# Graph layers with two gates on one core: 29 first additions of the gates as accumulating DMAs, and five smaller moves

## The chip, the cores and the metric

One NeuronCore of a Trainium2 chip runs the whole program. The metric is the device time of one execution in microseconds; the time before is the median of three runs, 809.16 us (806.93 to 809.22).

## What is computed

`x` has 256 nodes of 768 features. Four blocks follow each other, each as `x = x + block(relu(layernorm(x)))`: two relational graph layers with a gate behind each (L0), three relational graph layers (L1), a small attention network with an MLP (L2), and a two-layer attention network (L3). The change is almost wholly in the two gates of L0:

```python
def _gate(h, q, Wg, bg, Wq, bq):          # h: 8 x 32 nodes x 768, q: 8 x 64 x 768
    hg = jnp.einsum('bnf,gf->bng', h3, Wg[:, :F])
    qg = jnp.einsum('blf,gf->blg', q, Wg[:, F:]) + bg
    attn = jax.nn.sigmoid(hg[:, :, None, :] + qg[:, None, :, :])
    qi = jnp.einsum('bnlf,blf->bnf', attn, q)
    alpha = jax.nn.sigmoid(jnp.einsum('bnf,gf->bng', h3, Wq[:, :F])
                           + jnp.einsum('bnf,gf->bng', qi, Wq[:, F:]) + bq)
    return alpha * jnp.tanh(qi) + (1.0 - alpha) * h3
```

For each of 8 batches, 32 nodes, 64 query rows and 768 features one sigmoid is taken, multiplied by a query value and summed over the 64 rows.

## The kernel before

**A gate** (i = 0 after the first relational layer, i = 1 after the second) runs 48 steps. A step `s` takes 128 features of one batch, features on the partitions, and handles 32 nodes x 64 query rows = 2048 values, as two halves `u` of 1024 (32 rows `l` each):

- TensorE (`arguments`) makes hg + qg in PSUM with a selection matrix, two matmuls of 512 columns for each half.
- ScalarE (`sigmoid`, L864) writes the sigmoids of both halves to one of six product tiles, `slot_view(s)` (tile `s % 6`).
- VectorE (`gate_product`, L2050) multiplies all 2048 values by the query, which a copy holds in PSUM bank 6.
- GpSimd (`first_fold`, L640) adds the second half to the first: 1024 values are left. Step 47 alone is reduced by VectorE directly (L2057).
- What then happens is set for each step by a letter of `KIND[i]`. `V`: VectorE reduces 1024 values to 32 (`reduce`, L2072). `G`: GpSimd halves once more (`second_fold`, L646), VectorE reduces 512. `H`: GpSimd halves twice (L646, L649), VectorE reduces 256. `T`: TensorE adds in PSUM (`fold`, 8 calls of an identity matmul that appear as 16 rows of L1490), VectorE reduces 128.

Every engine works through its own list in order. The lists are written by hand in tables: `FOLD_AT[i]` (before which TensorE step a `T` is folded), `SECOND_AT[i]` (after which first addition GpSimd does a second one), `REST_AT[i]` (after which product VectorE does which reductions). `BY_DMA[i]` names steps whose first addition is made by a DMA that adds its source to its destination; before, both lists are empty. A product tile is free for step `s + 6` when its first addition is done (for half 1) and when it is reduced (for half 0); for a `T` the fold is enough.

**Beside the steps** TensorE makes the gate's own projections (`beside`): heads, query rows, `own` (h times Wq) and `query_part` (qi times Wq), which share two PSUM banks `acc`. They go to ScalarE and VectorE as high and low parts in `stage_hi` and `stage_lo`, from where SP's queue spreads them into `HQ` (`spread_heads`, `spread_queries`). At step 34 ScalarE takes the sigmoid of the first 128 nodes' update weight from `acc` into the SBUF tile `alpha` (`gate_alpha`, L883), VectorE multiplies (`gate_scale`, L2084), and GpSimd adds (`gate_add`, L655 or L658). From step 36 TensorE starts on `acc` anew with the other 128 nodes (`own(1, ...)`, bias matmul L1112). Their weight is handled behind step 47 (`last_half`, L2098).

**Weights** come as slabs of 768 KB through a ring of four, on SP's queue (L526), each issued when the slab four places ahead has been used. ScalarE's queue carries the vectors of the attention blocks, broadcast to all partitions (`av`, 2 MB, L915, issued at step 25 of the second gate), and the biases (L958) behind the second gate. `av` is first read behind the second relation of the third layer.

In L2's first attention layer VectorE makes two groups of columns of logit weights for the next layer (`logit_weights`, L2163 and L2167) between the two halves of `rows_lo(0, t)` (L2263), which TensorE's logits wait for.

## Time and profile before

| | |
|---|---|
| median of 3 runs | 809.16 us |
| profiled execution, its own time | 807.43 us |
| its span, first to last instruction | 805.6 us |
| first gate, steps from 114 to 262 us | 148 us |
| second gate, steps from 325 to 471 us | 146 us |
| TensorE matmul busy | 776.0 us (96%) |
| VectorE busy | 604.2 us (75%) |
| GpSimd busy | 508.5 us (63%) |
| ScalarE busy | 423.8 us (53%) |
| granted TensorE clock, mean | 0.999 |

The share of busy time over the span mixes the gates with the layers' products around them, which are bound otherwise. The gates have to be read by themselves: busy time of each engine within their two windows, the waits there, and the pace at which each engine goes from step to step. An instruction's mean duration in the list of groups includes a small overlap with the next one on its engine.

### The profile page before, as it was taken

The page shows a single profiled execution, that of the slowest core. Times are in us where ns is not written, and L with a number is a line of the kernel's source. Part 1 is how long each engine was busy: PE and PEld are TensorE (multiplying, and loading weights), DVE is VectorE, ACT ScalarE, POOL GpSimd, SP SyncE. Part 2 cuts the span into 40 slices and gives each one's busy share as a digit, 9 for nine tenths or more (in the row PEclk, how much of TensorE's full clock was granted, in tenths as well). Part 3 has the DMA queues.
Part 4 walks back from the last instruction along what each step waited for, and adds up shares of the span by engine and source line. Part 5 has one row for each costly group of instructions (what it writes and reads, how often), then busy time and mean ns, then how long its engine had stood idle before and what let it go on. Part 6 is the DMA issues. An engine that isn't in the chain of part 4 may idle for free.

```text
span 805.6 us, 10743 instructions
## 1 busy us (share of the span) xinstructions
PE 776.0 (96%) x4278; PEld 649.8 (81%) x4278; DVE 604.2 (75%) x664; ACT 423.8 (53%) x508; POOL 508.5 (63%) x216
## 2 busy tenths in 40 slices
PE   7999999999999999999999999999999999998998
PEld 4669995677756699667867768999999999975897
DVE  8966249999999740899999988564895498567454
ACT  6424446777675342677776734435442454253742
POOL 0535609999999274699999945750784177805500
PEclk9999999999999999999999999999999999999999
DMA  9037425445332474270344328465365446350001
GB/s 366 37 79 235 159 77 165 108 146 156 119 118 79 130 231 150 53 208 1 121 155 141 109 101 301 160 207 185 124 202 181 159 157 204 110 236 1 1 1 40
DMA packets 24410, 111.03 MB, mean 138 GB/s; under 512 B 3620, under 2 KB 6180, under 8 KB 23976
## 3 DMA queue, kind: packets, MB, share of 16 engines
q1 hardware_dynamic: 23240, 104.24, 39.9%
q10 hardware_dynamic: 1120, 6.10, 2.0%
q8 instruction: 34, 0.56, 0.3%
q14 instruction: 16, 0.13, 0.0%
HBM read 100.63 MB, written 0.79 MB: 126 GB/s over the span
## 4 chain that ended last, share of the span: by engine, by line
PE 68%; DVE 21%; POOL 4%; ACT 4%; issue 2%; DMA 0%; DVEq 0%; ACTq 0%
PE ps L1152 27%; DVE prod L2050 13%; PE ps L1118 10%; PE ps L1183 6%; PE ps L1443 5%; DVE qi_t L2072 4%; PE ps L1490 4%; PE ps L1665 3%; POOL w_lo L624 2%; PE ps L1310 2%; PE ps L1331 2%; ACT prod L864 2%; PE ps L1733 1%; PE ps L1311 1%; PE ps L1380 1%
## 5 line engine op out<-in xcount | busy, mean ns | idle before, releaser
L624 POOL TENSOR_TENSOR w_lo<-w_raw,w_hi 128x1536 fp32r<-128x1536 f32 x49 | 185.3, 3794 | 138.6 <-ACT w_hi L731 138.5
L640 POOL TENSOR_TENSOR prod<-prod 128x1024 f32<-128x1024 f32 x94 | 222.7, 2396 | 30.1 <-DVE prod L2050 29.8
L864 ACT ACTIVATE prod<-ps 128x1024 f32<-128x1024 f32 x192 | 185.8, 1024 | 64.9 <-PE ps L1443 63.8
L2050 DVE TENSOR_TENSOR prod<-prod,ps 128x2048 f32<-128x2048 f32 x96 | 216.9, 2281 | 1.4 <-ACT prod L864 1.0
L731 ACT ACTIVATE w_hi<-w_raw 128x1536 fp32r<-128x1536 f32 x60 | 88.9, 1487 | 119.0 <-PE ps L1152 108.6
L1443 PE MATMUL ps<-sel_pair,h_and_q 128*128 128x512 f32 x384 | 125.8, 442 | 10.5 <-ACT prod L864 9.8
L1152 PE MATMUL ps<-w_hi,yt_hi 128*128 128x384 f32 x480 | 122.9, 336 | 1.2 <-POOL w_lo L624 1.2
L1152 PE MATMUL ps<-w_lo,yt_hi 128*128 128x384 f32 x480 | 121.9, 334 | 0.0
L1152 PE MATMUL ps<-w_hi,yt_lo 128*128 128x384 f32 x480 | 121.8, 334 | 0.0
L1118 PE MATMUL ps<-w_raw,h_t 128*128 128x384 f32 x312 | 106.5, 486 | 0.0
L1443 PEld LDWEIGHTS ps<-sel_pair,h_and_q 128*128 128x128 f32 x384 | 66.6, 189 | 42.2 <-ACT prod L864 19.8
L1152 PEld LDWEIGHTS ps<-w_hi,yt_hi 128*128 128x128 f32 x480 | 85.4, 188 | 2.1 <-POOL w_lo L624 2.1
L1152 PEld LDWEIGHTS ps<-w_lo,yt_hi 128*128 128x128 f32 x480 | 86.8, 188 | 0.0
L1152 PEld LDWEIGHTS ps<-w_hi,yt_lo 128*128 128x128 f32 x480 | 86.7, 188 | 0.0
L1118 PEld LDWEIGHTS ps<-w_raw,h_t 128*128 128x128 f32 x312 | 58.7, 189 | 34.3 <-issue 0.2
L1937 DVE TENSOR_TENSOR ps<-ps,rinv 128x512 f32<-128x512 f32 x54 | 36.8, 695 | 55.9 <-PE ps L1183 55.3
L1490 PEld LDWEIGHTS ps<-prod,ident 128*128 128x128 f32 x544 | 65.8, 192 | 4.5 <-DVE qi_t L2072 0.4
L1490 PE MATMUL ps<-prod,ident 128*128 128x128 f32 x544 | 66.2, 275 | 0.0
L731 ACT ACTIVATE yt_hi<-ps 128x512 fp32r<-128x512 f32 (+1 forms) x58 | 35.0, 612 | 41.0 <-DVE ps L1937 40.6
L1924 DVE TENSOR_TENSOR w_lo<-w_raw,w_hi 128x1536 fp32r<-128x1536 f32 x11 | 20.9, 1904 | 43.5 <-ACT w_hi L731 43.3
L2072 DVE TENSOR_REDUCE qi_t<-prod 128x32 f32<-128x1024 f32 (+2 forms) x60 | 53.5, 901 | 0.0
L1183 PE MATMUL ps<-a,h_hi 128*128 128x256 f32 x192 | 48.1, 290 | 0.9 <-DVE yt_lo L1941 0.9
(263 smaller groups left out, 1110.0 us busy)
## 6 DMA issues: line engine op xcount, KB each, us to landing
w_raw<-weights SPq DMA_DIRECT2D x105, 768.0 KB, 4.4
wa_in<-weights SPq DMA_DIRECT2D x6, 768.0 KB, 5.9
w_gat<-weights SPq DMA_DIRECT2D x6, 768.0 KB, 9.2
w_query<-weights SPq DMA_DIRECT2D x3, 768.0 KB, 11.4
h_and_q<-stage_hi SPq DMA_DIRECT2D x24, 96.0 KB, 2.1
h_and_q<-stage_lo SPq DMA_DIRECT2D x24, 96.0 KB, 2.2
a_vec<-gat_vectors ACTq DMA_DIRECT2D x1, 2048.0 KB, 9.3
q_t<-queries ACTq DMA_DIRECT2D x1, 1536.0 KB, 10.3
```

What stands on the lines that cost most here:

```text
L624: pool.tensor_tensor(Wl[:, j, :], raw_slab(U, 0, j), Wh[:, j, :], ALU.subtract).then_inc(w_lo_by_pool, 1)
L640: pool.tensor_tensor(v[:, 0], v[:, 0], v[:, 1], ALU.add).then_inc(folded_once, 1)
L731: return act.activation(o, i, ACT.Copy)
L864: act.activation(slot_view(s)[:, u], args.rearrange("p b (n l) -> p (b n) l", l=LH), ACT.Sigmoid).then_inc(sigmoid_ready, 1)
L1118: return pe.matmul(ps[:, bank + h, 0:FH], left, raw_slab(U, c, k // 2)[:, o:o + FH], start=start, stop=stop)
L1152: mm = pe.matmul(ps[:, bank + h, 0:FH], Y[:, s, k, t * P:(t + 1) * P], Wx[:, j, c0:c0 + FH], start=False, stop=(last and k == KC - 1 and n ...
L1183: ins = pe.matmul(ps[:, 4 + j, kk * N:(kk + 1) * N], Hx[:, t, k * P:(k + 1) * P], A[:, t, v - 1, :], start=(n == 0), stop=(n == 3))
L1443: mm = pe.matmul(ps[:, bank + h, :], HQ[:, b, u, f * P:(f + 1) * P], SEL[:, h * 512:(h + 1) * 512], start=True, stop=True)
L1490: mm = pe.matmul(o, ident[:], slot_view(s)[:, 0, :, 4 * k:4 * k + 4], start=(k == 0), stop=(k == 7))
L1937: TT(tile3(j), tile3(j), inverse.unsqueeze(1).broadcast_to([P, 2, N]), ALU.mult).then_inc(sums_scaled, 1)
L2050: TT(slot_view(s), slot_view(s), query, ALU.mult).then_inc(products_ready, 1)
L2072: dve.tensor_reduce(qiT[:, f, b * NB:(b + 1) * NB], terms, AX.X, ALU.add).then_inc(qi_ready, 1)
```

## The change

- **29 first additions by DMA**: `BY_DMA` names 14 steps of the first gate and 15 of the second. GpSimd issues the DMA in place of the addition; who needs the result waits for the DMA's semaphore (`wait_folded`).
- **Sums dealt anew**: all tables. The kinds V, G, H, T number 17, 10, 6, 14 before and 11, 13, 11, 12 now in the first gate, 13, 10, 4, 20 before and 9, 12, 10, 16 now in the second. Of the steps that go by DMA, 9 and 6 are V, 2 and 3 G, 1 and 1 H, 2 and 5 T. Twenty of the 29 are reduced four products after their own, three (steps 1 and 3 of the first gate, 23 of the second) after three, and six (8, 30, 36 of the first gate, 17, 21, 30 of the second) after five.
- **Update weight in PSUM**: the sigmoid is written over its argument in `acc`, and VectorE multiplies from there; TensorE waits for that product before it starts on `acc` again. The tile `alpha` is gone.
- **Second pair of staging tiles** for the third group of query rows (`query_stage(2)`), at the addresses of `tq` and the former `alpha`; `gate_diff` therefore waits for the spread of that group.
- **Vectors' broadcast** at step 44 of the second gate instead of 25.
- **Logit weights of L2's second layer** in two calls, with `rows_lo(0, 1)` between them.

```diff
-BY_DMA = [(),
-          ()]
+BY_DMA = [(1, 3, 8, 11, 14, 19, 24, 27, 30, 34, 36, 38, 41, 44),
+          (3, 12, 14, 16, 17, 19, 21, 23, 25, 30, 33, 35, 38, 41, 44)]
...
-        alpha = sb("alpha", [P, F], F32, y_off + 15360)
+        second_lo = sb("second_stage_lo", [P, F], F32R, y_off + 12288)
+        second_hi = sb("second_stage_hi", [P, F], F32R, y_off + 15360)
...
+        def query_stage(r):
+
+            return (second_hi, second_lo) if r == 2 else (stage_hi, stage_lo)
...
-                if r == 2:
+                if r == 3:
                     act.wait_ge(lower_spread, 128)
-                if r == 3:
-                    act.wait_ge(query_spread[2], 128)
-                copy(halves(stage_hi[:]), two_banks(bank)).then_inc(staged_hi, 1)
+                copy(halves(query_stage(r)[0][:]), two_banks(bank)).then_inc(staged_hi, 1)
...
-                    act.activation(halves(alpha[:]), two_banks(acc), ACT.Sigmoid).then_inc(alpha_ready, 1)
+                    act.activation(two_banks(acc), two_banks(acc), ACT.Sigmoid).then_inc(alpha_ready, 1)
...
-                    if s == 25 and i == 1:
+                    if s == 44 and i == 1:
                         act.dma_start(av[:], gavec.partition_broadcast(P)).then_inc(vectors_in, 16)
...
                         if s == 36:
-                            pe.wait_ge(alpha_ready, 3 * i + 1)
+                            pe.wait_ge(alpha_diff_ready, 3 * i + 1)
...
-                    TT(tq[:], tq[:], alpha[:], ALU.mult).then_inc(alpha_diff_ready, 1)
+                    TT(halves(tq[:]), halves(tq[:]), two_banks(acc), ALU.mult).then_inc(alpha_diff_ready, 1)
...
-            logit_weights(1, raw_slab(30, 0, 1)[:, 0:2 * N], 0, 2, True)
+            logit_weights(1, raw_slab(30, 0, 1)[:, 0:2 * N], 0, 2, False, (0,))
             rows_lo(0, 1)
+            logit_weights(1, raw_slab(30, 0, 1)[:, 0:2 * N], 0, 2, True, (1,))
```

GpSimd's list in the first gate, from the first addition of step 7 on. `prod_N` is one of the six product tiles; before:

```order
L640 TENSOR_TENSOR prod_101<-prod_101 128x1024 [waits products_ready]
L646 TENSOR_TENSOR prod_101<-prod_101 128x32x16 [waits folded_once]
L640 TENSOR_TENSOR prod_102<-prod_102 128x1024 [waits products_ready]
L640 TENSOR_TENSOR prod_103<-prod_103 128x1024 [waits products_ready]
L640 TENSOR_TENSOR prod_104<-prod_104 128x1024 [waits products_ready]
L640 TENSOR_TENSOR prod_105<-prod_105 128x1024 [waits products_ready]
L646 TENSOR_TENSOR prod_105<-prod_105 128x32x16 [waits folded_once]
L649 TENSOR_TENSOR prod_105<-prod_105 128x32x8 [waits folded_twice]
```

and now:

```order
L646 TENSOR_TENSOR prod_102<-prod_102 128x1024 [waits products_ready]
L652 TENSOR_TENSOR prod_102<-prod_102 128x32x16 [waits folded_once]
L643 DMA prod_103<-prod_103 128x1024 [waits products_ready]
L646 TENSOR_TENSOR prod_104<-prod_104 128x1024 [waits products_ready]
L646 TENSOR_TENSOR prod_105<-prod_105 128x1024 [waits products_ready]
L652 TENSOR_TENSOR prod_105<-prod_105 128x32x16 [waits folded_once]
L655 TENSOR_TENSOR prod_105<-prod_105 128x32x8 [waits folded_twice]
L643 DMA prod_106<-prod_106 128x1024 [waits products_ready]
L652 TENSOR_TENSOR prod_103<-prod_103 128x32x16 [waits dma_folded2]
```

Steps 8 and 11 have become a DMA each, and the second addition of step 8 stands three first additions later, behind a wait for its transfer, with the rest of GpSimd's list behind it.

VectorE's list in the first gate around the scaling at step 34, before:

```order
L2050 TENSOR_TENSOR prod_104<-prod_104,ps 128x2048 [waits sigmoid_ready]
L2072 TENSOR_REDUCE qi_t<-ps 128x32 [waits fold_ready]
L2072 TENSOR_REDUCE qi_t<-prod_102 128x32 [waits folded_once]
L2084 TENSOR_TENSOR tanh_q<-tanh_q,alpha 128x768 [waits alpha_ready,diff_ready]
L2050 TENSOR_TENSOR prod_105<-prod_105,ps 128x2048 [waits sigmoid_ready]
```

and now:

```order
L2054 TENSOR_TENSOR prod_105<-prod_105,ps 128x2048 [waits sigmoid_ready]
L2076 TENSOR_REDUCE qi_t<-prod_102 128x32 [waits folded_thrice]
L2090 TENSOR_TENSOR tanh_q<-tanh_q,ps 128x768 [waits alpha_ready,diff_ready]
L2054 TENSOR_TENSOR prod_106<-prod_106,ps 128x2048 [waits sigmoid_ready]
L2076 TENSOR_REDUCE qi_t<-ps 128x32 [waits fold_ready]
```

One short reduction instead of two stands ahead of the scaling, and the scaling's second operand is in PSUM.

TensorE's list at step 36 of the first gate, where `acc` is started anew, before:

```order
L1443 MATMUL ps<-sel_pair,h_and_q 128x512
L1112 MATMUL ps<-bias,sel_row 128x384 [waits alpha_ready]
L1112 MATMUL ps<-bias,sel_row 128x384
L1118 MATMUL ps<-w_raw,h_t 128x384 [waits w_landed0]
L1118 MATMUL ps<-w_raw,h_t 128x384 x2
```

and now:

```order
L1447 MATMUL ps<-sel_pair,h_and_q 128x512
L1116 MATMUL ps<-bias,sel_row 128x384 [waits alpha_diff_ready]
L1116 MATMUL ps<-bias,sel_row 128x384
L1122 MATMUL ps<-w_raw,h_t 128x384 [waits w_landed0]
L1122 MATMUL ps<-w_raw,h_t 128x384 x2
```

The same matmuls now wait for VectorE's scaling, no longer for ScalarE's sigmoid; the sigmoid arguments of step 37 stand behind them.

## Rows read from the trace of the kernel before

**Rows 1.** Windows: length; busy PE, PEld, DVE, ACT, POOL; clock; DMA share; GB/s.
```profile
114.00:262.00 148.00, 141.62 (x646) 101.43 (x645) 147.01 (x110) 102.70 (x115) 137.68 (x70) 1.00 0.42 121
325.00:471.00 146.00, 138.69 (x695) 102.39 (x693) 143.02 (x114) 103.91 (x117) 135.73 (x68) 1.00 0.36 110
262.00:283.00 21.00, 20.65 (x100) 14.77 (x101) 14.44 (x19) 8.34 (x11) 6.07 (x2) 1.00 0.46 144
```
**Rows 2.** Groups by form, first gate: count, busy, mean ns, idle before.
```profile
L640 POOL TENSOR_TENSOR prod<-prod 128x1024 f32<-128x1024 f32 x47 | 110.8, 2390 | 22.1 <-DVE prod L2050 21.9
L646 POOL TENSOR_TENSOR prod<-prod 128x512 f32<-128x512 f32 x16 | 21.3, 1328 | 1.3
L649 POOL TENSOR_TENSOR prod<-prod 128x256 f32<-128x256 f32 x6 | 4.4, 736 | 0.5
L2072 DVE TENSOR_REDUCE qi_t<-prod 128x32 f32<-128x1024 f32 x17 | 20.6, 1213 | 0.0
L2072 DVE TENSOR_REDUCE qi_t<-prod 128x32 f32<-128x512 f32 x10 | 6.7, 676 | 0.0
L2072 DVE TENSOR_REDUCE qi_t<-prod 128x32 f32<-128x256 f32 x6 | 2.5, 415 | 0.0
L2072 DVE TENSOR_REDUCE qi_t<-ps 128x32 f32<-128x128 f32 x14 | 4.0, 287 | 0.0
L2084 DVE TENSOR_TENSOR tanh_q<-tanh_q,alpha 128x768 f32<-128x768 f32 x1 | 2.0, 2035 | 0.0
L1975 DVE TENSOR_TENSOR stage_lo<-ps,stage_hi 128x768 fp32r<-128x768 f32 x3 | 2.9, 952 | 0.0
```
**Rows 3.** The same view, second gate.
```profile
L640 POOL TENSOR_TENSOR prod<-prod 128x1024 f32<-128x1024 f32 x47 | 111.9, 2403 | 8.0 <-DVE prod L2050 7.9
L2072 DVE TENSOR_REDUCE qi_t<-ps 128x32 f32<-128x128 f32 x20 | 5.8, 288 | 1.9 <-PE ps L1490 1.9
L2084 DVE TENSOR_TENSOR tanh_q<-tanh_q,alpha 128x768 f32<-128x768 f32 x1 | 1.2, 1182 | 0.0
L629 POOL TENSOR_TENSOR small<-small,mhalf 128x1 f32<-128x1 f32 x1 | 0.6, 570 | 0.0
```
**Rows 4.** Timeline of TensorE, first gate: start, duration, one fold and its step.
```profile
178.47 1.95 PE L1490 MATMUL ps<-prod,ident 128*128 128x128 f32 x16
180.18 1.18 PE L1443 MATMUL ps<-sel_pair,h_and_q 128*128 128x512 f32 x4
```
**Rows 5.** DMA issues of the page: KB each, median us from issue to landing.
```profile
w_raw<-weights SPq DMA_DIRECT2D x105, 768.0 KB, 4.4
a_vec<-gat_vectors ACTq DMA_DIRECT2D x1, 2048.0 KB, 9.3
g_bias<-gat_biases ACTq DMA_DIRECT2D x1, 1536.0 KB, 6.1
```
**Rows 6.** Timeline of SP's queue, the spread of the first heads.
```profile
119.65 0.68 SPq L548 DMA_DIRECT2D h_and_q<-stage_hi  x1
...
129.91 0.60 SPq L548 DMA_DIRECT2D h_and_q<-stage_lo  x1
```
**Rows 7.** Timelines of TensorE and VectorE at step 36, second gate.
```profile
427.56 0.51 PE L1112 MATMUL ps<-bias,sel_row 128*128 128x384 f32 x2
...
427.79 1.18 DVE L2084 TENSOR_TENSOR tanh_q<-tanh_q,alpha 128x768 f32<-128x768 f32 x1
```
**Rows 8.** Timelines: ScalarE at step 44, second gate; a slab load; its use by TensorE.
```profile
453.27 1.96 ACT L864 ACTIVATE prod<-ps 128x1024 f32<-128x1024 f32 x2
...
460.19 0.33 SPq L526 DMA_DIRECT2D w_raw<-weights  x1
...
472.46 2.74 PE L1118 MATMUL ps<-w_raw,h_t 128*128 128x384 f32 x8
```
**Rows 9.** Timelines of VectorE and TensorE in L2's first attention layer.
```profile
715.21 0.28 DVE L2263 TENSOR_TENSOR logit_rows<-ps,logit_rows 40x128 fp32r<-40x128 f32 x1
...
715.55 0.48 PE L1700 MATMUL ps<-sel_dst,logit_rows 128*128 128x512 f32 x1 [0.46 <-DVE logit_rows L2263]
```

40 lines of the change are left out of this document (22 added, 18 removed), and 10 rows, old and new, of the table REST_AT.

## Prediction

> **What bounds the kernel now.** I read the windows of the gates first. VectorE is busy 147.0 of the first gate's 148 us and 143.0 of the second's 146; TensorE 141.6 and 138.7; GpSimd 137.7 and 135.7 [rows 1]. The reader is to see three nearly full engines with VectorE ahead. A cut on one engine is therefore worth only what the other two let through, and has to be made on all three. The groups by form tell what a sum costs on each: VectorE reduces a V in 1.213 us, a G in 0.676, an H in 0.415, a T in 0.287; GpSimd's first addition takes 2.390, a second 1.328, a third 0.736 [rows 2]. A fold lengthens TensorE's step by 180.18 - 178.47 = 1.71 us [rows 4]. A step takes 148/48 = 3.08 us on average. The granted clock stays at 1.00 throughout [rows 1], so the 2.4 GHz level is not in question.
>
> **VectorE.** First gate: six V fewer, three G more, five H more, two T fewer: -7.28 + 2.03 + 2.08 - 0.57 = -3.7 us [rows 2]. Second: four V fewer, two G and six H more, four T fewer. With the same durations and 0.288 for a T [rows 3], that is -4.85 + 1.35 + 2.49 - 1.15 = -2.2 us. The scaling at step 34 has both operands in SBUF and takes 2.035 us in the first gate, 1.182 in the second [rows 2, 3]. With one operand in PSUM, the nearest row of its size takes 0.952 [rows 2]. So -1.1 and -0.2 us. Together: **-4.8 and -2.4 us**.
>
> **TensorE.** Two and four folds fewer: 2 x 1.71 = -3.4 and 4 x 1.71 = -6.8 us. In the first gate TensorE has 6.4 us free, so this mainly keeps it from becoming the bound. In the second VectorE is idle 3.0 us, of which 1.9 are waits for folds [rows 1, 3]; with a fifth fewer folds and the other engines shorter I take back 1.0 us of it (between 0 and 1.9).
>
> **GpSimd.** Without the price of issuing: first gate, 14 first additions fewer, eight second and five third ones more: -33.5 + 10.6 + 3.7 = -19.2 us. Second: 15 fewer, eight and six more, by the same rows: -35.8 + 10.6 + 4.4 = -20.8 us. What an accumulating DMA holds GpSimd for is in no row. From below, GpSimd's smallest operation, 128x1, takes 0.57 us [rows 3]; from above, the addition that it replaces, 2.39. SP's queue holds its engine 0.60 us for one transfer [rows 6]. I take 0.57 + 0.60 = 1.17 us, near the lower end, since writing a list of 128 rows touches far less than adding 131,072 values. Then GpSimd changes by -19.2 + 14 x 1.17 = -2.8 and -20.8 + 15 x 1.17 = -3.3 us. It breaks even at 19.2/14 = 1.37 and 20.8/15 = 1.39 us; its free 10 us per gate [rows 1], about half of them ahead of the first product, cover a little more. The Trainium skill (DMA: Bandwidth & Descriptors, Latency and other measured facts) puts GpSimd's emission at about 1 us; no row shows it, and by it GpSimd would gain 5.2 and 5.8 us, with the sum unchanged because VectorE sets it.
>
> **Landing.** A transfer has a source and a destination of 512 KB each and reads both and writes one: 1536 KB. The row with that many bytes landed after 6.1 us; 768 KB took 4.4, 2048 KB 9.3 [rows 5]. I take 6.1, with 4.4 and 9.3 as bounds. GpSimd is up to 1.3 us behind, by one second addition, and issues for 1.17: ready 8.6 us behind the product. Reduced four products later it has 4 x 3.08 = 12.3 us, three later 9.2. So 26 of 29 are hidden even at 9.3 (11.8 us). The three with lag three are not, at that end, and step 1 of the first gate meets the 16 spread transfers of 119.65 to 130.51 [rows 6]. Product tiles come free for the sigmoids of six steps later, so the same slack covers ScalarE. Seven second additions now wait for a DMA, with the rest of GpSimd's list behind them. Three stand three products after their own, four (34 and 41 of the first gate, 14 and 33 of the second) only two: 2 x 3.08 + 1.17 = 7.3 us, just what issue and landing take together. At 9.3 us those four hold GpSimd 3.2 us each, 6.4 per gate, about its free time. For the three short lags and these four I charge **+0.8 us** together (0 to 3 x 2.6 = 7.8). The skill (same page, Anatomy of one DMA — SWDGE (gpsimd) path) gives 2.0 us plus bytes over 436e3. For 512 KB that would be an estimated 3.2 us, and 5.6 for 1536 KB; no row has a transfer of this kind. By either the 0.8 would fall to 0.
>
> **The other parts.** TensorE's new wait at step 36: in the second gate it started the bias matmul at 427.56, and the scaling began at 427.79 [rows 7]. Ending 0.95 us later it would hold TensorE for 427.79 + 0.95 - 427.56 = 1.2 us, and the sigmoid arguments of step 37 behind it. But of the reductions ahead of it in VectorE's list a T and a G are gone there (a T and a V, for an H, in the first gate), 0.29 + 0.68 us; that leaves **+0.2 us** (0 to 1.2 in each gate), and VectorE is two products away from needing those arguments. `last_half` gets its factor from PSUM: some 0.1 us per product, behind which TensorE is busy 20.65 of 21.00 us [rows 1]; 0. The second pair of staging tiles takes away waits that do not occur before; 0, and the new wait of the difference at step 29 is for transfers issued some 15 steps earlier. The broadcast: ScalarE comes to step 44 at 453.27 [rows 8]; from about 454 2 MB land in 9.3 us alone [rows 5], beside the slab of 460.19, which TensorE needs at 472.46 [rows 8]; even both in a row, 4.4 + 9.3 = 13.7 us from 454, are there by 468. Its first reader stands behind the second relation of the next layer. 0 us, and what it did at step 25 is also hidden. The logit split: `rows_lo` need not wait for the second half of the weights, and TensorE's idle 0.46 us before the logits goes [rows 9]: **-0.4 us**.
>
> **Sum.** -4.8 - 2.4 - 1.0 + 0.8 + 0.2 - 0.4 = -7.6 us on the profiled execution's 807.43 us (span 805.6 and 1.8 around it): 799.8. That execution is 1.7 us below the median of 809.16, so against the median 801.6; I say **802**.
>
> **Rivals.**
> *A, the forecast*: VectorE keeps the lead and gains show. For it: the three engines' cuts are of like size. Best case, issue below 1.2, no late landing, all 3.0 us of idle in the second gate gone: -4.8 - 5.4 - 0.4 = -10.6, 798.5; worst, 3 us more of waits than charged: 804.6.
> *B, GpSimd eats the gain*: at 1.6 us per issue it is +3.2 us longer in both gates (-19.2 + 22.4, -20.8 + 24.0). It starts some 5 us into the gate and has perhaps 3 us of slack there, so the gates end within 1 to 2 us of where they do now: against the median again 807 to 811. That price lies between the row of 0.57 and the row of 2.39, so it can't be excluded.
> *C, GpSimd becomes the bound and the kernel is slower*: one mechanism, the issue of an accumulating DMA in GpSimd's list, from about 1.6 us up. At 2.0 us GpSimd has +8.8 and +9.2 us; less 3 to 5 us of slack each, +9 us together: 818. Against it: SP's 0.60 per transfer.
> *D, late landings*: the DMA engines add at a lower rate than they copy. It decides where landing, waiting and issue exceed 12.3 us, so from 12.3 - 2.5 = 9.8 us. At 10.5 us 26 transfers cost 0.7 each and three 3.8: +30 on top of -8: 831. For it: slab loads and additions meet on engines already 0.42 and 0.36 busy [rows 1], and four of GpSimd's second additions have no slack beyond 6.1 us. Against it: no copy row is that slow.
> That the change does not do what it says is excluded: GpSimd's list has the 29 DMAs in place of the additions.
>
> **Chances.** A measurement of this kernel tells 0.3% (2.4 us) from no change. A 0.69, of which 0.66 faster and 0.03 within; B 0.11 within; C 0.11 and D 0.09 slower. So 0.66 faster, 0.14 the same, 0.20 slower. The range reaches from 797.5 (A's best case and a little of the runs' own spread) up through B to the near part of C: 797.5 to 813. D and the far part of C are left out, about 0.14, and 0.04 below.
>
> **What would show it.** The first gate takes 144 us and the second 142 to 143. VectorE is still busy over 98% of the first. A V among the DMA steps shows no wait of VectorE for a DMA, except at steps 1 and 3 of the first gate. The DMA queue of GpSimd shows 29 issues of 512 KB with a landing near 6 us, and GpSimd's rows leave gaps of about 1.2 us where they stand. The scaling takes 0.95 us. Wrong would be: gaps of 1.6 us and more on GpSimd with VectorE waiting for second additions (B, C), VectorE, TensorE's folds or ScalarE waiting for DMA (D), or a gate that is shorter by less than VectorE's sum although nothing waits.

## The result, and the profile after

| | before | after |
|---|---|---|
| median of the runs, us | 808.03 (806.93 to 809.22, 5 runs) | 802.16 (800.89 to 805.78, 5 runs) |
| ratio to before, 95% interval | | 0.9929 [0.9908, 0.9950] |
| profiled execution, us (span) | 807.43 (805.6) | 805.78 (804.0) |

The change gives 5.9 us, 0.7%. The profiled execution of after is its slowest, and where its 3.6 us over the median are lost stands below; the gates can be read in it all the same. First the windows of the two gates, cut at the same two instructions in both kernels (columns: length; busy PE, PEld, DVE, ACT, POOL; clock; DMA share; GB/s). Before:

```profile
114.07:262.36 148.29, 141.87 (x647) 101.69 (x648) 147.30 (x110) 102.63 (x115) 137.68 (x70) 1.00 0.42 121
325.85:471.34 145.49, 138.18 (x691) 102.17 (x692) 142.74 (x113) 103.11 (x115) 134.88 (x68) 1.00 0.36 111
```

After:

```profile
115.03:260.19 145.16, 139.34 (x615) 98.11 (x616) 142.97 (x110) 102.31 (x115) 130.44 (x83) 1.00 0.69 174
323.64:466.99 143.35, 132.86 (x628) 94.33 (x628) 140.74 (x113) 103.27 (x115) 126.60 (x82) 1.00 0.66 167
```

The gates are 3.1 and 2.1 us shorter. VectorE's busy time fell by 4.3 and 2.0 us, so its idle time went from 1.0 to 2.2 us in the first gate and from 2.75 to 2.6 in the second. GpSimd fell by 7.2 and 8.3 us, TensorE by 2.5 and 5.3. The groups of the first gate, as [rows 2] (count, busy, mean ns, idle before):

```profile
L2054 DVE TENSOR_TENSOR prod<-prod,ps 128x2048 f32<-128x2048 f32 x48 | 108.6, 2283 | 2.0 <-ACT prod L868 1.8 <-ACT ps L737 0.2
L646 POOL TENSOR_TENSOR prod<-prod 128x1024 f32<-128x1024 f32 x33 | 79.5, 2413 | 25.3 <-DVE prod L2054 24.7
L652 POOL TENSOR_TENSOR prod<-prod 128x512 f32<-128x512 f32 x24 | 31.4, 1310 | 1.6
L643 POOL DMA_DIRECT2D prod<-prod x14 | 12.3, 878 | 0.0
L2090 DVE TENSOR_TENSOR tanh_q<-tanh_q,ps 128x768 f32<-128x768 f32 x1 | 1.0, 951 | 0.0
```

The same of the second gate, as [rows 3]:

```profile
L646 POOL TENSOR_TENSOR prod<-prod 128x1024 f32<-128x1024 f32 x32 | 77.8, 2436 | 11.6 <-DVE prod L2054 11.3
L643 POOL DMA_DIRECT2D prod<-prod x15 | 13.3, 888 | 1.3 <-DVE prod L2054 1.1 <-issue 0.2
L2076 DVE TENSOR_REDUCE qi_t<-prod 128x32 f32<-128x1024 f32 x9 | 10.9, 1212 | 1.4 <-DMA prod<-prod 1.4
L2076 DVE TENSOR_REDUCE qi_t<-ps 128x32 f32<-128x128 f32 x16 | 4.6, 285 | 0.3 <-PE ps L1494 0.3
```

An issue holds GpSimd for 0.88 us. GpSimd waits 24.7 us for products in the first gate, 19.7 of them ahead of the first one, so 5.0 inside it, and 11.3 in the second (7.9 before [rows 3]). The line of the issues says who waited for their landings and how long these take:

```profile
  DVE qi_t L2076: 1.4, 1
...
DMA to landing us min/median/max: 4.5/5.2/9.3
```

One wait in 29. It is the sum of step 23 of the second gate, issued at 392.69 (GpSimd's timeline, first row) and reduced at 400.72 with a lag of three (VectorE's):

```profile
392.69 0.85 POOL L643 DMA_DIRECT2D prod<-prod  x1
...
400.72 1.22 DVE L2076 TENSOR_REDUCE qi_t<-prod 128x32 f32<-128x1024 f32 x1 [1.39 <-DMA prod<-prod]
```

What the chain of waits runs through has changed hands, in both gates. The first gate, from 120 to 260 us, by line, before:

```profile
by line: DVE prod L2050 58.2%; DVE qi_t L2072 16.6%; PE ps L1118 8.8%; PE ps L1443 4.2%; ACT prod L864 3.2%; issue 3.1%; DVE qi_t L2057 1.6%; DVE tanh_q L2084 1.4%; PE ps L1490 1.3%; DVE stage_lo L1975 1.2%; DVE tanh_q L2078 0.7%; ACT stage
```

and after:

```profile
by line: PE ps L1122 35.5%; PE ps L1447 22.8%; PE ps L1494 14.2%; ACT prod L868 8.0%; issue 5.2%; DVE prod L2054 4.8%; POOL prod L646 3.4%; DVE qi_t L2076 1.7%; DVE qi_t L2061 1.6%; POOL prod L652 0.9%; POOL prod L655 0.5%; PE ps L1322 0.5%
```

VectorE's products and sums made three quarters of it before; now TensorE's gate products, sigmoid arguments (L1447) and folds do. VectorE is still busy 98.5% of this gate (142.97 of 145.16 us), so the two are about equally long, and neither leads by much. The second gate, from 330 to 466 us, before and after:

```profile
by line: PE ps L1118 24.2%; PE ps L1490 19.8%; PE ps L1443 19.2%; DVE prod L2050 14.6%; ACT prod L864 7.8%; POOL prod L640 5.2%; issue 4.6%; DVE qi_t L2072 2.9%; DVE stage_lo L1975 0.7%; ACT a L731 0.6%; PE ps L1112 0.5%; ACT stage_hi L731 
...
by line: DVE prod L2054 39.5%; DVE qi_t L2076 10.2%; PE ps L1122 7.6%; PE ps L1494 6.7%; PE ps L1447 6.1%; DMA prod<-prod 5.9%; POOL prod L646 5.3%; ACT prod L868 4.8%; issue 4.2%; POOL prod L652 2.9%; DVE qi_t L2061 1.6%; POOL prod L643 1.
```

Here it went the other way: before, TensorE's work made 63% of the chain, and with four folds fewer VectorE's products and sums make half of it, with 6% of waits for the new DMAs.

Behind the gates this execution loses time to something the change does not touch. VectorE stands 3.4 us for a load of logit weights and so starts its product 0.16 us behind GpSimd's `w_lo`; the product takes 5.0 us in place of the 1.76 that it takes alone, and TensorE waits for the `w_lo` that VectorE owes it. Behind that wait TensorE's granted clock is at its 1.2 GHz level from 618.6 to 622.0 (timelines of GpSimd, VectorE and TensorE, and the window, with the columns of above):

```profile
603.27 3.50 POOL L630 TENSOR_TENSOR w_lo<-w_raw,w_hi 128x1536 fp32r<-128x1536 f32 x1 [3.51 <-ACT w_hi L737]
...
603.43 4.96 DVE L2170 TENSOR_TENSOR wa_tmp<-wa_in,a_vec 128x1536 f32<-128x1536 f32 x1 [3.44 <-DMA wa_in<-weights]
...
617.16 0.62 PE L1156 MATMUL ps<-w_hi,yt_hi 128*128 128x384 f32 x2 [2.98 <-DVE w_lo L1928]
...
618.60:622.00 3.40, 3.40 (x13) 3.40 (x12) 0.00 (x0) 0.81 (x1) 0.00 (x0) 0.50 0.56 209
```

Before, the same product started 0.16 us ahead of GpSimd's `w_lo` (607.46 and 607.62) and took 1.76 us; TensorE waited 1.24 us at that place, for GpSimd, and its clock stayed at 1.00.

### The profile page after: what moved, and what is told of

Same layout as the page of the kernel before. It is cut to its first block, busy times and chain, and to the rows that moved or that the text cites. A ratio compares the mean times of both kernels' runs of the same rounds, so it can differ in the third digit from the quotient of the medians.

```text
span 804.0 us, 10573 instructions
## 1 busy us (share of the span) xinstructions
PE 770.6 (96%) x4182; PEld 640.3 (80%) x4182; DVE 599.6 (75%) x664; ACT 423.5 (53%) x508; POOL 490.8 (61%) x243
## 4 chain that ended last, share of the span: by engine, by line
PE 70%; DVE 15%; POOL 5%; ACT 4%; DMA 2%; issue 2%; DVEq 0%; SPq 0%; ACTq 0%
PE ps L1156 26%; PE ps L1122 12%; DVE prod L2054 8%; PE ps L1447 6%; PE ps L1187 5%; PE ps L1494 4%; PE ps L1669 3%; ACT prod L868 2%; DVE qi_t L2076 2%; PE ps L1314 2%; PE ps L1335 2%; POOL prod L646 1%; POOL w_lo L630 1%; PE ps L1737 1%; PE ps L1315 1%
## 5 line engine op out<-in xcount | busy, mean ns | idle before, releaser
L630 POOL TENSOR_TENSOR w_lo<-w_raw,w_hi 128x1536 fp32r<-128x1536 f32 x49 | 183.2, 3749 | 145.1 <-ACT w_hi L737 145.0
L646 POOL TENSOR_TENSOR prod<-prod 128x1024 f32<-128x1024 f32 x65 | 157.3, 2424 | 37.0 <-DVE prod L2054 36.0
L1447 PE MATMUL ps<-sel_pair,h_and_q 128*128 128x512 f32 x384 | 127.7, 445 | 13.0 <-ACT prod L868 12.1
L1447 PEld LDWEIGHTS ps<-sel_pair,h_and_q 128*128 128x128 f32 x384 | 66.6, 189 | 48.3 <-ACT prod L868 23.9
L652 POOL TENSOR_TENSOR prod<-prod 128x512 f32<-128x512 f32 x46 | 61.2, 1330 | 3.1
L1494 PEld LDWEIGHTS ps<-prod,ident 128*128 128x128 f32 x448 | 53.9, 192 | 4.6 <-issue 0.9
L1494 PE MATMUL ps<-prod,ident 128*128 128x128 f32 x448 | 54.8, 275 | 0.3 <-POOL prod L646 0.2
L1928 DVE TENSOR_TENSOR w_lo<-w_raw,w_hi 128x1536 fp32r<-128x1536 f32 x11 | 19.7, 1795 | 44.6 <-ACT w_hi L737 44.4
L2076 DVE TENSOR_REDUCE qi_t<-prod 128x32 f32<-128x256 f32 (+2 forms) x66 | 48.7, 756 | 1.4 <-DMA prod<-prod 1.4
```

Source lines behind the costliest of these rows:

```text
L630: pool.tensor_tensor(Wl[:, j, :], raw_slab(U, 0, j), Wh[:, j, :], ALU.subtract).then_inc(w_lo_by_pool, 1)
L646: pool.tensor_tensor(v[:, 0], v[:, 0], v[:, 1], ALU.add).then_inc(folded_once, 1)
L652: pool.tensor_tensor(v[:, :, 0:16], v[:, :, 0:16], v[:, :, 16:32], ALU.add).then_inc(folded_twice, 1)
L1447: mm = pe.matmul(ps[:, bank + h, :], HQ[:, b, u, f * P:(f + 1) * P], SEL[:, h * 512:(h + 1) * 512], start=True, stop=True)
L1494: mm = pe.matmul(o, ident[:], slot_view(s)[:, 0, :, 4 * k:4 * k + 4], start=(k == 0), stop=(k == 7))
L2076: dve.tensor_reduce(qiT[:, f, b * NB:(b + 1) * NB], terms, AX.X, ALU.add).then_inc(qi_ready, 1)
```

## The experiments

As the length of a gate I take, in each profile, the time from the start of its first product to the start of the difference behind its last sum (VectorE's timeline). Medians stand beside those of the kernel before from the same runs.

| kernel | median, before's | ratio [95%] | gate 1, 2 |
|---|---|---|---|
| before | 808.03 | | 145.09, 142.27 |
| after | 802.16, 808.03 | 0.9929 [0.9908, 0.9950] | 141.95, 140.13 |
| e1 four edits | 808.37, 807.55 | 1.0016 [0.9999, 1.0033] | 144.31, 143.56 |
| e1b three edits | 806.70, 807.74 | 0.9994 [0.9982, 1.0006] | 145.06, 142.26 |
| e2 deal, no DMAs | 831.62, 807.55 | 1.0308 [1.0291, 1.0325] | 156.79, 154.24 |
| e3 24 DMAs, old deal | 815.37, 807.55 | 1.0109 [1.0093, 1.0126] | 149.83, 144.45 |
| e3b 19 DMAs, old deal | 810.42, 808.03 | 1.0029 [1.0014, 1.0045] | 145.82, 145.40 |
| e4 issue + 0.84 us | 806.12, 807.55 | 0.9991 [0.9978, 1.0003] | 143.54, 142.72 |
| e4b issue + 1.35 us | 821.71, 807.74 | 1.0169 [1.0154, 1.0184] | 152.36, 149.95 |
| e5 one staging pair | 801.56, 807.74 | 0.9925 [0.9905, 0.9945] | 142.42, 140.29 |
| e6 weight in SBUF | 802.99, 807.74 | 0.9937 [0.9917, 0.9957] | 142.24, 140.09 |
| e7 earlier `wa_in` | 800.75, 808.03 | 0.9908 [0.9892, 0.9925] | 141.92, 140.45 |
| e8 more on GpSimd | 812.20, 808.03 | 1.0053 [1.0037, 1.0069] | 147.23, 145.47 |
| e9 e7 + one step later | 799.93, 807.94 | 0.9903 [0.9887, 0.9920] | 141.94, 139.92 |

### The small edits without DMAs and deal (e1, e1b)

```diff
-KIND = ["HVGVGTGGGTHVHTVGTTHVTGTHVHTVGGTHVVHGTGVHTGHTVGH",
...
+KIND = ["GVHVVTGGTVTHVTHTVVTTHVHTGGTVVHTTVVGGVVTGVTGTGVH",
...
```

All five tables of numbers are those of before; the rest of the change stays.

> The changed kernel's code with the tables of before and no accumulating DMA: what is left of the change is the update weight in PSUM, the second pair of staging tiles, the broadcast of the vectors at step 44 and the split of the logit weights. Theory (the gain of 5.9 us comes for the most part from the 29 DMAs and the new deal of the sums, which need each other): these four give 1.0 to 2.0 us, from the two scalings of VectorE (2.035 and 1.182 us before, 0.95 after) and 0.4 us behind the attention, so 806 to 807 beside 808.0. Rival (the deal only moves work about, and the gain is that of the scalings, of the freed staging tile and of the later broadcast): 803 or less.

Measured: 808.37, 0.8 us over before (the interval just reaches no change), so the theory's 1 to 2 us of gain are not there. The first gate is 0.8 us shorter, the second 1.3 us longer. The timeline of TensorE in the second gate of e1:

```profile
427.80 0.62 PE L1116 MATMUL ps<-bias,sel_row 128*128 128x384 f32 x2 [1.04 <-DVE tanh_q L2090]
...
433.05 1.95 PE L1494 MATMUL ps<-prod,ident 128*128 128x128 f32 x16
```

And of VectorE:

```profile
426.80 0.94 DVE L2090 TENSOR_TENSOR tanh_q<-tanh_q,ps 128x768 f32<-128x768 f32 x1
...
435.03 0.29 DVE L2076 TENSOR_REDUCE qi_t<-ps 128x32 f32<-128x128 f32 x1 [2.30 <-PE ps L1494]
```

TensorE now waits 1.04 us at step 36 for the scaling (it waited for nothing there before [rows 7]); everything queued behind it moves by that, and the fold of 433.05 comes 2.30 us late for VectorE. e1b puts the weight back into SBUF, with TensorE waiting for the sigmoid alone, and leaves the other three edits:

```diff
-TT(halves(tq[:]), halves(tq[:]), two_banks(acc), ALU.mult)
+TT(tq[:], tq[:], alpha[:], ALU.mult)
-pe.wait_ge(alpha_diff_ready, 3 * i + 1)
+pe.wait_ge(alpha_ready, 3 * i + 1)
```

> The kernel of the four edits without DMAs (old tables), but with the update weight in SBUF: the second staging pair, the broadcast at step 44 and the split of the logit weights are left. In the profile of the four edits TensorE waits 1.04 us for the scaling at step 36 of the second gate and VectorE then 2.30 us for a fold, and the gate is 1.3 us longer than before while the first is 0.8 us shorter. Theory (the weight in PSUM cost 1.3 us in the second gate by that wait): the second gate is back at 142.3 us between its first product and the tanh's difference, the first at 145.1, and the whole at 807 to 807.5 beside 808.4 with the four. Rival (the second gate's loss comes from the broadcast at step 44 or the staging tiles): it stays at 143.5, and the whole is at 808.5 or more.

Measured: 806.70, and both gates at before's length to 0.03 us. So the weight in PSUM took that 1.3 us, and the second staging pair and the broadcast at step 44 are worth nothing in the gates. What is left, some 1 us on the medians, lies behind them, where the split of the logit weights is; 1.0 us of two medians is hardly more than their scatter, the interval includes no change, and the split was not run by itself.

### The deal without DMAs (e2)

```diff
-BY_DMA = [(1, 3, 8, 11, 14, 19, 24, 27, 30, 34, 36, 38, 41, 44),
-          (3, 12, 14, 16, 17, 19, 21, 23, 25, 30, 33, 35, 38, 41, 44)]
+BY_DMA = [(), ()]
```

> The changed kernel with its new tables, but all first additions on GpSimd again. GpSimd gets 14 additions of 2.41 us in place of 14 issues of 0.88 us in the first gate (+21 us) and 15 in the second (+23 us), and had 5.0 and 11.3 us of waiting for products there. Theory (GpSimd's load is what the DMAs pay for): it becomes what sets the time in both gates, +16 and +12 us, so about 830 (822 to 832). Rival (GpSimd's waits hide much of it, since VectorE and TensorE set the pace): under 815.

Measured: 831.62. VectorE's waits in the second gate of e2 (total us, times, longest):

```profile
DVE qi_t L2076 <- POOL prod L655: 5.3, 2, 4.2
DVE qi_t L2076 <- POOL prod L652: 3.3, 2, 2.1
```

and GpSimd has next to nothing left of its waits for products (5.3 us, 4.8 of them ahead of the gate's first). The deal alone costs 24 us; it can only be had with the DMAs. Not all of the 24 us is GpSimd's own time. TensorE's granted clock is at its 1.2 GHz level in four stretches of the two gates (about 161.6 to 165.0, 260.5 to 267.4, 431.2 to 434.6 and 472.2 to 475.6 us), each behind a wait of TensorE of 2.0 to 4.7 us, as here for GpSimd:

```profile
261.68 3.75 PE L1494 MATMUL ps<-prod,ident 128*128 128x128 f32 x16 [3.90 <-POOL prod L646]
```

The fold takes 3.75 us in place of 1.95. By my estimate, half of the 17 us at that level, up to 8.5 of the 24 us are the clock's.

### DMAs without the deal (e3, e3b)

The other four tables are those of before.

```diff
-BY_DMA = [(), ()]
+BY_DMA = [(1, 4, 10, 13, 17, 20, 22, 26, 28, 30, 36, 38),
+          (3, 9, 12, 15, 17, 20, 26, 28, 30, 33, 35, 44)]
```

> The changed kernel's code with the tables of before, and 24 of its first additions (12 in each gate, all of sums that are reduced three or more steps later) by accumulating DMAs. VectorE and TensorE keep their loads of before in the gates; only GpSimd is relieved, by 12 x 1.5 = 18 us per gate. Theory (before, VectorE set the time in the first gate and VectorE with TensorE in the second; GpSimd did not): within 1.5 us of the kernel with the four edits alone, so 804.5 to 807. Rival (GpSimd was late often enough that its relief pays by itself): 802 or less, at which the new deal would add nothing.

Measured: 815.37. Both theories were wrong: taking 18 us per gate off GpSimd cost 8 us. From the chain of waits of its first gate:

```profile
131.20 8.89 DMA prod<-prod
159.54 6.23 DMA prod<-prod
189.59 3.73 DMA h_and_q<-stage_lo
```

TensorE's timeline at the third:

```profile
193.38 2.07 PE L1447 MATMUL ps<-sel_pair,h_and_q 128*128 128x512 f32 x4 [2.30 <-DMA h_and_q<-stage_lo]
```

And SP's queue, which issues the queries' spread while the additions of steps 20 and 22 are being issued at 179.19 and 185.98:

```profile
186.31 0.58 SPq L544 DMA_DIRECT2D h_and_q<-stage_hi  x1
186.94 0.76 SPq L545 DMA_DIRECT2D h_and_q<-stage_lo  x1
187.74 1.81 SPq L544 DMA_DIRECT2D h_and_q<-stage_hi  x1
189.59 1.61 SPq L545 DMA_DIRECT2D h_and_q<-stage_lo  x1
```

The last two issues take 1.8 and 1.6 us where the six before them took 0.5 to 0.8 (and all eight 0.5 to 0.6 in the kernel before), so the spread takes SP 7.7 us in place of 5.3, lands late, and TensorE and VectorE (2.63 us) stand for it. Behind its wait TensorE's granted clock is at 0.50, the 1.2 GHz level, until about 196.7, and the four matmuls of 193.38 take 2.07 us in place of 1.18. In after, steps 20 to 23 of the first gate have no DMA: its issues fall at 177.35 and 191.67, on either side of the spread.

e3b keeps clear of the spread, takes only sums with four or more steps in the first gate (but for step 36, which is reduced after three), and has the weight in SBUF, so that it is e1b plus 19 DMAs:

```diff
-BY_DMA = [(), ()]
+BY_DMA = [(10, 13, 15, 19, 26, 30, 36, 38),
+          (3, 9, 12, 15, 17, 20, 26, 30, 33, 35, 44)]
```

> The tables of before with 19 accumulating DMAs (8 and 11), the update weight in SBUF: so the kernel of 806.7 us (second staging pair, broadcast at step 44, split logit weights) plus DMAs alone. In the run with 24 DMAs on the old tables the first gate was 4.7 us longer than before: its queries' spread landed late (DMAs of steps 20 and 22 beside the spread of steps 21 to 23; TensorE waited 2.9 us for it and VectorE 2.6 behind it) and DMAs of steps with a lag of three landed after 6.2 to 8.9 us. Here no DMA is issued between steps 20 and 25 of the first gate and its eight sums have four or more steps. Theory (that loss was landing times and the collision; GpSimd's relief by itself buys nothing on the old tables): the first gate at 144.5 to 145.5 and the second at 142 to 143 us between first product and tanh's difference, the whole at 806 to 807.5. Rival 1 (DMA traffic slows the gates wherever it lies): 809 and above. Rival 2 (the relief does pay once nothing collides): under 804.5.

Measured: 810.42. The collision is gone and the first gate back to 145.82, but the second is 3.1 us longer than e1b's. TensorE's timeline there:

```profile
367.18 3.54 PE L1497 MATMUL ps<-prod,ident 128*128 128x128 f32 x16 [1.17 <-DMA prod<-prod]
```

VectorE's:

```profile
370.76 0.29 DVE L2079 TENSOR_REDUCE qi_t<-ps 128x32 f32<-128x128 f32 x1 [2.47 <-PE ps L1497]
...
431.10 2.58 DVE L2093 TENSOR_TENSOR tanh_q<-tanh_q,alpha 128x768 f32<-128x768 f32 x1
```

A late landing holds a fold, the fold holds VectorE, and the scaling takes 2.58 us where it took 1.20 in e1b. The fold itself takes 3.54 us in place of 1.95: from about 366.9 to 370.4, behind TensorE's wait, the granted clock is 0.50, the 1.2 GHz level, so more of VectorE's 2.47 us comes from the clock than from the landing. The two make up the gate's 3.1 us: beside e1b VectorE is idle 1.7 us longer (4.3 for 2.6) and busy 1.4 us longer, of which the scaling is 1.38. That leaves nothing in the second gate for rival 1, a cost wherever the DMAs lie; the first gate's 0.8 us over e1b are not explained. My theory had counted VectorE's waits only and had no price for a fold, which is wanted earlier than a reduction. So the DMAs alone give nothing.

### The price of an issue (e4, e4b)

```diff
 pool.dma_start(v[:, 0], v[:, 1], accum_op=ALU.add).then_inc(dma_folded[s % PSLOTS], 16)
+pool.tensor_tensor(pad[:], half, half, ALU.add).then_inc(padded, 1)
```

`half` is a constant column broadcast to 208 elements and `pad` is read by nobody. e4 has the line once behind each issue, e4b twice.

> The changed kernel with one GpSimd operation of about 0.6 us more behind each of the 29 DMA issues, so that an issue costs 0.88 + 0.6 = 1.5 us, near the 1.6 us at which the prediction had GpSimd eat the gain. GpSimd gets 8.4 us more in the first gate and 9.0 us more in the second, against waits for products of 5.0 and 11.3 us. Theory (those waits are slack that can be used): +3 to +4 us in the first gate and 0 to +1 in the second, so about 806 (804 to 808). Rival (the waits are where GpSimd has to be on time, and its slack is none): 8 us or more in each gate, 816 and above. Other rival (TensorE and VectorE set the time everywhere, and GpSimd has more slack than its waits show): within 1 us of 802.2.

Measured: 806.12. The operation took more than I had said; GpSimd's groups of e4:

```profile
L647 POOL DMA_DIRECT2D prod<-prod x29 | 25.8, 890 | 1.1 <-DVE prod L2064 1.1
L653 POOL TENSOR_TENSOR pad<-mhalf 128x208 bf16<-128x208 f32 x29 | 24.3, 839 | 0.0
```

With 1.7 us per issue the kernel is 4.0 us over after (+1.6 and +2.6 in the gates), for 24.3 us more of work on GpSimd. Its 1.4 us under before are not clear of noise.

> The changed kernel with two more GpSimd operations behind each issue. With one, of 0.82 us, GpSimd lost 11.5 us more in the first gate and 12.3 in the second, and the kernel 3.9 us. With two an issue takes 0.88 + 1.64 = 2.5 us. Theory (the waits for products were GpSimd's slack, and now it is used up): 20 us or more on top of the 806.1 us of one operation would be all of it (23.8); the second is paid at 70% or more, so 823 to 830. Rival (GpSimd still has slack, since its results are wanted steps later): under 818.

Measured: 821.71; the operations' group of e4b:

```profile
L653 POOL TENSOR_TENSOR pad<-mhalf 128x208 bf16<-128x208 f32 x58 | 39.2, 676 | 2.3
```

The two take 1.35 us together, not 1.64, so the "all of it" of my expectation is 14.9 us and not 23.8. Of these 14.9 us the kernel pays 15.6. The first 24 us on GpSimd are paid at a sixth, the next 15 in full. Between an issue of 1.7 and one of 2.2 us the kernel passes from 1.4 us under before to 14 over; where between 0.9 and 2.2 us the cost begins to rise, three points do not tell. Nor is "in full" all GpSimd's: in e4b TensorE waits for its addition, and the granted clock falls to 0.50 (about 254.2 to 261.0 us, and again 462.4 to 465.9), which it does not in e4's gates:

```profile
255.80 3.75 PE L1504 MATMUL ps<-prod,ident 128*128 128x128 f32 x16 [3.54 <-POOL prod L656]
```

Half of those 10.3 us, up to 5 of the 15.6, are the clock's by my estimate.

### Single edits undone in after (e5, e6)

e5 gives the queries one pair of staging tiles again:

```diff
-return (second_hi, second_lo) if r == 2 else (stage_hi, stage_lo)
+return stage_hi, stage_lo
```

> The changed kernel with one pair of staging tiles for the queries again, and ScalarE's two waits for their spreads as before. The prediction put the second pair at 0. Theory (it hides nothing in this deal either): within 0.8 us of the changed kernel, so 801.5 to 803. Rival (the 29 DMAs delay the spreads that share the DMA engines, so that the single pair comes free late, at steps 13 and 21 of the first gate): 3 us or more, 805 and above, with a wait of ScalarE or VectorE for a spread of the queries.

Measured: 801.56, 0.6 us under after's 802.16: the second pair is worth nothing here either.

e6 is after with the weight in SBUF, by the lines of e1b:

> The changed kernel with the update weight in its SBUF tile again, and TensorE at step 36 waiting for the sigmoid alone. The scaling of VectorE takes 1.2 to 2.0 us in place of 0.95 in each gate. Theory (VectorE is late there, but TensorE is freed of its wait for the scaling): +0.3 to +1.3 us, so 802.5 to 803.5. Rival (what is gained on VectorE is lost on TensorE, and the edit is worth nothing): 801.5 to 802.5. The third case, that the edit costs more than it gives here too: under 801.

Measured: 802.99, with gates of 142.24 and 140.09: as after's within 0.3 us; six runs from 800.86 to 805.55 leave the 0.8 us of the medians unclear. The scaling itself is the surprise. It has both operands in SBUF and does not take 1.2 to 2.0 us (VectorE's instructions on the tile, min/median/max):

```profile
L2093 DVE TENSOR_TENSOR tanh_q<-tanh_q,alpha x2: 949/950/952, 218.7 to 424.0; 128x768 f32<-128x768 f32 x2
```

GpSimd's timeline beside the one of 218.7:

```profile
213.82 4.92 POOL L647 TENSOR_TENSOR prod<-prod 128x1024 f32<-128x1024 f32 x2 [0.29 <-DVE prod L2057]
218.76 0.87 POOL L644 DMA_DIRECT2D prod<-prod  x1
219.75 1.83 POOL L662 TENSOR_TENSOR h<-h,tanh_q 128x768 f32<-128x768 f32 x1
```

GpSimd's addition ends at 218.74, just as the scaling begins, and while the scaling runs GpSimd only issues. In e3b GpSimd was adding from 430.49 to 432.86, and the same instruction ran from 431.10 to 433.68: it ended 0.82 us behind the addition. So it did, to 0.01 us, in all four cases in which it began inside an addition whose end the timelines show (the first gates of before, e1b and e3b, and this one), so that it pays for what is left of the addition. In the new deal the scaling falls on the end of an addition, with the issue of a DMA behind it, in both gates (218.71 and 424.05), and that gives what the move to PSUM was to give. Whether the DMA is needed for it or the moment alone does it, no run separates.

### Towards a faster version (e8, e7, e9)

e8 gives GpSimd more of VectorE's sums, into the waits that it shows in after:

```diff
-KIND = ["HVGVGTGGGTHVHTVGTTHVTGTHVHTVGGTHVVHGTGVHTGHTVGH",
-        "VVHVGTTHTTTGTTHTTTHVGTHVHVHTGGTHGGTVTGGGVGHTVHG"]
+KIND = ["HVGVGTGGGTHGHTVGTTHGTGTHGHTVGGHHVVHGTGGHTGHTVGH",
+        "VVHGGTTHTTTGTTHTTTHGGTHVHGHTGGTHGGTGTGGGVGHTVHG"]
```

The four sums of each gate that turn from V to G (11, 19, 24, 38; 3, 19, 25, 35) get their second addition three steps behind their own, one step ahead of the reduction, which stays where it was. In the first gate step 30 turns from T to H, its second addition at step 34 and its reduction at 35, and step 33 gets a DMA and is reduced at 37; in the second, step 23 is reduced at 27.

> The changed kernel with a further deal, to beat both: eight sums whose first addition is a DMA and which VectorE reduced from 1024 (1.21 us) get their second addition on GpSimd (1.33 us) and are reduced from 512 (0.68 us), four in each gate; one sum of the first gate goes from TensorE's fold to GpSimd (1.3 + 0.7 us there, 1.95 us off TensorE); step 33 of the first gate becomes a DMA with a lag of four; step 23 of the second gate, the one VectorE waited 1.4 us for, is reduced a step later. GpSimd gets 5.9 us more in the first gate (4 x 1.33 + 2.06 - 1.5) and 5.3 in the second; with 11.5 and 12.3 us more the gates lost 1.6 and 2.6 us. VectorE gets 2.1 us less in the first gate and 2.1 plus the wait of 1.4 in the second. Theory (VectorE sets most of both gates): -1 us in the first gate, -2 in the second, so 799 (797.5 to 800.5). Rival (TensorE's loop of arguments and sigmoid has become as long, so that VectorE's gain turns into waits for it): 801 to 802.5.

Measured: 812.20, 10 us over after. VectorE's timeline of e8, at three of the moved sums:

```profile
188.86 0.69 DVE L2062 TENSOR_REDUCE qi_t<-prod 128x32 f32<-128x512 f32 x1 [2.54 <-POOL prod L638]
...
398.16 0.69 DVE L2062 TENSOR_REDUCE qi_t<-prod 128x32 f32<-128x512 f32 x1 [3.58 <-POOL prod L638]
...
418.38 0.69 DVE L2062 TENSOR_REDUCE qi_t<-prod 128x32 f32<-128x512 f32 x1 [3.45 <-POOL prod L638]
```

VectorE waits 5.9 us in the first gate and 9.0 in the second for such additions. GpSimd had the time, but not there: the second addition comes a step before its reduction, behind another sum's additions in the same list (at 188.86 it had also waited 0.70 us for its own DMA). In e4 twice as much work, spread over 29 places and wanted by nobody, cost 4.0 us. Neither my theory nor the rival named this; I had taken a sum of waits for room.

e7 issues two loads of logit weights one unit of weights earlier:

```diff
-WA_AT = (16, 19, 21, 24, 26, 28)
+WA_AT = (16, 18, 21, 23, 26, 28)
```

> The changed kernel with two of the six loads of logit weights issued one unit of weights earlier on SyncE's queue. VectorE waited 2.04 us at 524.7 and 3.44 us at 603.4 of the changed kernel's profile for them, and TensorE behind the second 3.3 us for a w_lo of VectorE. Theory (in most executions TensorE is busy throughout there, so that these waits cost nothing, and only single executions show the loss): 801 to 802.3, within 0.5 us. Rival (they cost about 1 us in each run): 800.8 or less.

Measured: 800.75, with all six runs between 800.51 and 801.28, where after had 800.89 to 805.78 and e5 and e6 reached 806.04 and 805.55. By its number this is the rival's case, if only by 0.05 us; the median moves by 1.4 us against after's five runs, and the executions of 804 to 806 do not occur. What the quicker executions gained is not shown: e5's and e6's profiles (801.24, 801.60) have no wait of TensorE of 1 us there. VectorE's timeline in the layer where after's profile lost its time:

```profile
600.28 1.75 DVE L2170 TENSOR_TENSOR wa_tmp<-wa_in,a_vec 128x1536 f32<-128x1536 f32 x1
...
603.85 4.90 DVE L2170 TENSOR_TENSOR wa_tmp<-wa_in,a_vec 128x1536 f32<-128x1536 f32 x1
```

No wait for the load, and TensorE has no wait from 595 to 620; the product of 4.90 us beside GpSimd's `w_lo` is a later one, for which nobody stands. That after's times of 804 to 806 us came from the late load is borne out by two more profiles. e4's (809.59 us, median 806.12) and e2's (834.85, median 831.6) are of executions 3.2 to 3.5 us above the medians, and of all profiles only they and after's have the product behind the load start 0.05 to 0.16 us after GpSimd's `w_lo` (5.0 to 5.1 us), TensorE's wait of 3.0 us for VectorE's `w_lo`, and the clock of 0.50 behind it. Where the product starts first it takes 1.76 us. One execution of e6 (804.49 us at a mean clock of 1.000) does not fit, so there may be a second cause.

e9 adds to it the one sum that was late, a step later:

```diff
-           (15,), (16,), (), (17, 18), (19,), (20,), (), (21, 22, 23), (24,), (26,), (25,), (), (27, 28, 29), (), (), (),
+           (15,), (16,), (), (17, 18), (19,), (20,), (), (21, 22), (24, 23), (26,), (25,), (), (27, 28, 29), (), (), (),
```

> The changed kernel with the two earlier loads of logit weights (800.75 us), and with the sum of step 23 of the second gate reduced a step later, behind the product of step 27: it is the one sum with a DMA and a lag of three steps for which VectorE waited in every profile (1.2 to 1.6 us, its landing takes 8 us or more there). Nothing else is moved. Theory (VectorE sets the pace at that place): 0.8 to 1.4 us less, so 799.4 to 800. Rival (TensorE's loop is as long there, and VectorE's wait only moves into its wait for the sigmoid or the turn of the queries behind it): 800.4 to 800.9.

Measured: 799.93 (799.61 to 800.36), 8.0 us under before and 2.2 under after, with all four executions under e7's six: it beats both. VectorE's timeline behind that step:

```profile
399.31 2.29 DVE L2040 TENSOR_TENSOR prod<-prod,ps 128x2048 f32<-128x2048 f32 x1 [0.81 <-ACT prod L854]
```

The wait for the DMA (1.18 us in e7) is gone, and 0.81 us of it has come back as a wait for the sigmoid; the gate gained 0.5 us, of the 0.8 us between the medians. The theory's number holds and the rival's mechanism is seen at work too.

## Why the prediction was right, and where its terms were off

The forecast was 802 against a median of 809.16, a gain of 7.6 us in the sum; the runs give 802.16 and a gain of 5.9 against 808.03. That 802 was met to 0.2 us is luck: the kernel before came out 1.1 us faster than the median that I had, and the gain 1.7 us smaller than its sum. The direction, the size to a quarter and most of rival A hold; A's "VectorE keeps the lead" does not, in the first gate. Term by term:

- **VectorE, -4.8 and -2.4 us**: busy time fell by 4.3 and 2.0. The reductions of the first gate come to 33.8 - 30.1 = 3.7 us less, as worked out, and the scalings to 0.95 us; of what is missing in the second, 0.5 us is an operation of the norm, 128x1, that took 0.63 us in place of 0.15. The -1.1 for the scaling was right in size and wrong in its cause: e6 shows that in the new deal, where no addition of GpSimd's runs beside it, it is had without PSUM; and on the old deal (e1) the wait that comes with PSUM costs more than it gives.
- **-1.0 us of VectorE's idle time in the second gate**: this is the step that failed, by a term too good and not by a wrong mechanism. The waits for folds did go (1.9 to 0.3 us), but 1.4 us for a DMA and 0.7 for the sigmoid took their place, 2.75 to 2.6 us in all. In the first gate, where I had put nothing, idle time grew by 1.2 us: VectorE waits 1.8 us for ScalarE's sigmoid. The chain of waits there runs through TensorE from 140 to 237 us and no longer through VectorE, so TensorE's loop of arguments and sigmoid has become as long; I had counted on TensorE's cut keeping it from that (its busy time fell by 2.5 and 5.3 us, where two and four folds at 1.71 us made 3.4 and 6.8). With the +0.8 and +0.2 for new waits I had VectorE's idle time unchanged over both gates; it grew by 1.1 us. That VectorE is ahead, on which the sum rests, held in the first gate only; in the second the chain ran through TensorE, so there the cut of its folds was a condition of the gain as much as VectorE's own. The 1.1 us and the 0.9 us of missing cuts are the gates' 5.3 us in place of 7.2.
- **Landing, +0.8 us**: measured 5.2 us in the middle and 9.3 at most, beside the 6.1 taken and the bounds of 4.4 and 9.3; the only wait is 1.4 us, at one of the three lags of three. I had named steps 1 and 3 of the first gate for it, where there was none. The four second additions without slack did not wait.
- **Issue, 1.17 us**: 0.88. GpSimd's cut is 7.2 and 8.3 us in place of 2.8 and 3.3, and it bought nothing: GpSimd's waits for products inside the second gate grew from 3.1 to 6.5 us, and e8 shows that they are no room. The Trainium skill (DMA: Bandwidth & Descriptors, Latency and other measured facts) put it at about 1 us, nearer than my estimate. For the landing, its formula (same page, Anatomy of one DMA — SWDGE (gpsimd) path) gave an estimated 3.2 us for 512 KB and 5.6 for 1536; the trace's 5.2 us is near the second and rules out the first.
- **TensorE's wait at step 36, +0.2 us**: none in after, where the scaling ends at 219.20 and 424.50 and the bias matmul starts at 219.46 and 425.20. On the old deal my bound of 1.2 us was met in the second gate, where e1 shows 1.04 us on TensorE and 2.30 on VectorE (0.73 of these were there before). That the reductions which the new deal took away ahead of the scaling hide it is read from the lists, 0.97 us in the second gate; no run puts them back alone.
- **Staging pair, broadcast 0**: e5 and e1b bear it out. **Logit split, -0.4 us**: from ScalarE's write of `h` ahead of L2's first attention layer (709.35 before, 708.39 after) to the end of the span, 96.25 us before and 95.61 after, one profile each.
- **Rivals B and C**: e4 is B's case at 1.7 us per issue and 1.4 us under before, where I gave 2 under to 2 over for 1.6. e4b is C's at 2.25 us: C's working gives 12.3 + 13.0 - 9 = +16 us there, and it measured +14. That e4b comes so near is in part luck, since C had no term for the clock. Both mechanisms are real; the issue costs half of what they need.
- **Rival D** did not come about in after, but e3 and e3b are its case: with landings of 5.7 and 5.4 us in the middle, much below the 9.8 us that I had asked for. It does not take a slow middle, only one landing of 8 to 9 us at a sum that is wanted early (e3b's fold waits for the transfer issued at 359.27, until 367.18), or issues into a spread.

## What to carry to other kernels

- Work that is moved to a free resource gives nothing by itself. Here relief alone (e3b beside e1b, with 19 DMAs at the steps that the old deal allows) and the deal alone (e2) cost 4 and 24 us; together they gain 5 us over e1b (e6, which differs from e1b in them alone, has gates 2.8 and 2.2 us shorter), because the deal spends the relief on the engine that leads and keeps late results away from early readers.
- Idle time in an engine's list is room only if it lies between the moment an input is there and the moment its result is wanted. e4 adds 24 us of work to the same engine and costs 4 us, e8 adds 11 and costs 10.
- A wait of TensorE can cost more than itself. Look at the granted clock behind each wait of some us before its cost is put down to the engine that was late: in e3b the clock held the fold longer than the late transfer did.
